# Sorted row numbers kept as integers, and two weight loads issued by another engine

## The chip, the cores and the metric

The kernel runs on one core of a Trainium2 chip. The metric is device time in microseconds of one execution. A core has five engines that each run their own list of instructions in order: TensorE (matrix products; PE in the rows, its weight loads PEld), VectorE (DVE), ScalarE (ACT), GpSimd (POOL) and SyncE (SP), which here does nothing but issue transfers and wait for their conditions. Engines meet only at semaphores. A transfer (DMA) is issued by SyncE, ScalarE or GpSimd and raises a semaphore by 16 once it has landed; 16 DMA engines carry it.

## The reference, cut to what matters

`x` is 16 sequences of 512 tokens of 128 numbers, 8192 tokens in all. Two layers follow each other:

```python
xn = layernorm(x)
x = x + cosformer_attention(xn) + moe_0(xn)        # 16 heads; shared + 16 routed experts, top 4 as a dense gate
xn = layernorm(x)
x = x + rope_causal_attention(xn) + moe_1(xn)      # 16 heads of 8; 8 experts, top 1

def moe_1(h):                                      # what the change touches
    route = softmax(h @ router_w + router_b)       # 8 experts
    best, p = argmax(route), max(route)
    for e in range(8):
        a, g = split(h @ w1[e], 2)                 # w1[e]: 128 x 1024
        y = (silu(a) * g) @ w2[e]                  # w2[e]: 512 x 128
        out = where(best == e, y, out)
    return out * p
```

## The kernel before, in words

The kernel keeps `x` on the chip and walks over the 16 sequences, called batches. A first part (up to about 540 us of the profile) computes layer 0 for each batch, the second norm, the queries, keys and values of layer 1, and the routing of layer 1. A second part (from about 580 us) computes the causal attention of layer 1 batch by batch; mixed into it run the experts of layer 1, as 71 tiles of 128 rows.

**Sorting rows to experts.** A token's row goes to one expert only, so the rows are sorted by expert in a table in memory, `xs`. A row of `xs` has 130 numbers: the 128 of the normalized token, its row number in the output (column `D`), and its probability (column `D + 1`). VectorE's `ranks` works out the place of each row (`slotu`) and writes the row numbers, which it holds in `token`, into column `D` of `xn[1]` (L1166). GpSimd's `sort` then writes 128 rows at a time with an indirect transfer, four for each batch, 64 in all (L1345). `pads` fills the ends of the experts' lists with rows of zeros (`zeros`), whose row number `NOROW` is outside the output, so that nothing is written for them. After the last of the 64 has landed, VectorE works out the tables of the tiles (`tables`, L1225 to L1257), each tile's expert and first row.

**A tile of experts**, number `n`, passes through these stages, each named by a function on the engine that does it:
- `load` on SyncE (L1500 to L1513): 128 rows of `xs` go to one of `U` = 6 buffers `xsb[:, u]`, with `u = n % 6`. From tile 6 on it first waits until the buffer is free.
- `rows` on GpSimd (L1348 to L1353): the row numbers, floats in column `D`, are cast to integers in `rowu`.
- `staged` on ScalarE copies the expert's first weights out of `w1` to `w1s`; `turned` on TensorE transposes the rows (L771), and ScalarE copies them to `xsT` (L964).
- `hidden` on TensorE (L779), ScalarE and VectorE: the first product, and silu(a) * g.
- `outputs` on TensorE (L790) with `w2`; VectorE scales by the probability into `ysb` (L1277); GpSimd adds the 128 rows to the output with an indirect transfer, the scatter, whose row numbers come from `rowu` (L1365). Its landing raises `d_ys{u}`.

**Attention.** Of each batch, `max` on TensorE and VectorE finds row maxima, group by group (four groups of four heads, counted from 0). TensorE transposes them (L721), ScalarE and VectorE split them in a high and a low half (`mrows` L924, `mlow` L1190), and SyncE's `mlow` sends both halves to the query tile with two transfers (L1447). The scores of the group wait for that (L731). ScalarE takes the exponential (L934), GpSimd masks the diagonal (L1333), TensorE multiplies by the values (L746). SyncE's `relay` (L1454 to L1476) brings the next batch's queries and keys into place, beginning with two transfers of zeros at L1468, once per batch. GpSimd's `add` adds a finished batch to the output (L1374), after as many tiles' scatters as `among(b)` says.

**The order.** Every stage has a place on a common scale, a batch taking 20 units. The places are written out by hand (`FIRST`, `SECOND`, `ATTENTION`, `CLOSING`, `END`), and those of the tile stages are derived from `tile(n)` in `LAST`: for instance `load` of tile `n + U` stands at `tile(n + 1) + 0.3` and `outputs` of tile `n` at `tile(n + 1) + 0.15`. There are nine tiles for two batches, at uneven places. `stages()` sorts all by place, and each engine runs, in that order, the stages that it has a function for. An engine that waits in one stage holds back all its later ones.

**The second experts' weights** arrive in two loads, both issued by SyncE before the change: `w1` (4 MB, at place 65.65, into the space `early` that layer 0 has used, so after its last use) and `w2` (2 MB, at place 87.5, into the space of layer 0's small tiles).

Of the kernel before, what the change touches and what calls it, by code (L numbers as in the profile page):

```python
# [13 lines left out]
U32 = mybir.dt.uint32  # L14
AX_X = mybir.AxisListType.X

P = 128
B, L, D = 16, 512, 128
# [15 lines left out]
U = 6  # L34
# [230 lines left out]
    casts=[-166.65],  # L265
    rest=[-217.1])


TPB, TBS, TB0 = 9, 2, 1
AHEAD = 5  # L270
TILES = placed(
    tile=[67.65, 76.4, 77.45, 84.2, 84.85, 87.65, 96.35, 97.4, 105.75])

# [7 lines left out]

def among(b):

    return min(NTILE, TPB * b // TBS + AHEAD)


def tile(n):
    return S2 * (TB0 + TBS * (n // TPB)) + TILES[n % TPB][0]


LAST = [(tile(n + 1) + 0.3, "load", n + U) for n in range(NTILE - U)]
LAST += [(tile(n - 1) - 0.5, "staged", n) for n in range(NTILE)] + [(tile(n - 1) + 0.3, "rows", n) for n in range(NTILE)]
LAST += [(tile(n - 1) - 0.15, "turned", n) for n in range(NTILE)] + [(tile(n), "hidden", n) for n in range(NTILE)]
LAST += [(tile(n + 1) + 0.15, "outputs", n) for n in range(NTILE)]

# [85 lines left out]
def once(names):  # L381
# [11 lines left out]
    "mean0 mean1 gated kvr kv px gate at0 x1 xl logits rope low onehot base slots mlow sub0 sub1 "  # L393
    "max heads x2 tables rowzero silu glu chain "

    "fills kept var0 var1 less0 less1 rstd0 rstd1 shift0 shift1 qs rotated rows "

    "d_x d_nextx d_big d_w d_wup d_wq d_wrest d_restx d_gate d_gates0 d_gates1 d_relayq d_relayk d_relayed d_vout d_vload d_sorted d_mrows0 d_mrows1 d_w1 d_w2 d_pad d_begun d_out"
) + [f"d_{kind}{u}" for kind in ("xs", "ys") for u in range(U)]
# [6 lines left out]
def place(nc, ctx, io):  # L406
# [101 lines left out]
    m.w2 = sb("w2", [P, E1 * FC * D])  # L508
    m.ti = sb("ti", [P, 4, E1 + 1], I32)
    m.tf = sb("tf", [P, 6, E1 + 1])  # L510
    m.rowu = sb("rowu", [P, U], U32)
    m.jr = sb("jr", [P, 4, NTAB])
    m.ji = sb("ji", [P, 3, NTAB], I32)
    m.xsb = sb("xsb", [P, U, D + 2])
# [284 lines left out]
            share[name](b, i)  # L799


def scalar_program(nc, m, s, order, work):
    act = nc.scalar

    def wk(stage, n=0):
# [142 lines left out]

    def staged(_, n):
        if n == 0:
            act.wait_ge(s["tables"], 1)
            act.wait_ge(s["d_w1"], 16)
        off = act.value_load(m.ji[0:1, 0, n:n + 1], min_val=0, max_val=(E1 - 1) * 2 * F1)
        if n >= WS:
            act.wait_ge(s["hg_mm"], n - WS + 1)
        act.copy(m.w1s[:, n % WS, :], m.w1[:, bass.ds(off, 2 * F1)]).then_inc(s["staged"], 1)  # L958
# [13 lines left out]
    def casts(_, i):  # L972
        act.wait_ge(s["d_wrest"], 16 * NWREST)
        act.copy(m.wo1[:, :], m.o16[:, :]).then_inc(s["casts"], 1)

    share = dict(casts=casts, norm0=norm0, norm1=norm1, xnT0=xnT0, kvr=kvr, up=up, q=q, kv=kv, route0=route0, gT=gT, at0T=at0T, down=down, xnT1=xnT1, parts=parts,
                 v=v, vst=vst, route1=route1, mrows=mrows, score=scores, sums=sums, mT=mT, staged=staged, turned=turned,
                 hidden=hidden)
    for name, b, i in order:
# [4 lines left out]
def vector_program(nc, m, s, order, work):  # L984
# [169 lines left out]
    def ranks(b, i):  # L1154
        ps = wk(("ranks", b, i))
        dve.wait_ge(s["ranks_mm"], b + 1)
        dve.wait_ge(s["onehot"], b + 1)
        then(dve.tensor_tensor(m.rk[:, :, :], ps[:, 0:NT * E1].rearrange("p (t e) -> p t e", t=NT),
                               m.base[:, :].unsqueeze(1).to_broadcast([P, NT, E1]), ALU.add))
        dve.tensor_tensor(m.base[:, :], m.base[:, :], ps[:, NT * E1:(NT + 1) * E1], ALU.add).then_inc(s["base"], 1)  # L1160
        then(dve.tensor_tensor(m.rk[:, :, :], m.rk[:, :, :], m.oh[:, :, :], ALU.mult))
        dve.tensor_scalar(m.token[:, :], m.token[:, :], float(L), None, ALU.add)
        then(dve.tensor_reduce(m.s1[:, 2, :], m.rk[:, :, :], AX_X, ALU.add))
        if b:
            dve.wait_ge(s["d_sorted"], 16 * NT * b)
        dve.tensor_copy(m.xn[1][:, :, D], m.token[:, :])  # L1166
        dve.tensor_copy(m.slotu[:, b * NT:(b + 1) * NT], m.s1[:, 2, :]).then_inc(s["slots"], 1)  # L1167

    def maxima(b, i):
# [118 lines left out]
def pool_program(nc, m, s, order, work):  # L1288
# [56 lines left out]
        pool.indirect_dma_start(m.xs_d, at, m.xn[1][:, t, :], None).then_inc(s["d_sorted"], 16)  # L1345


    def rows(_, n):  # L1348
        u = n % U
        pool.wait_ge(s[f"d_xs{u}"], 16 * (n // U + 1))  # L1350
        if n >= U:
            pool.wait_ge(s[f"d_ys{u}"], 16 * (n // U))
        pool.tensor_copy(m.rowu[:, u:u + 1], m.xsb[:, u, D:D + 1]).then_inc(s["rows"], 1)  # L1353

    def outputs(_, n):
        u = n % U
        pool.wait_ge(s["ycopy"], n + 1)
        pool.wait_ge(s["rows"], n + 1)
        if n == 0:
            pool.wait_ge(s["d_begun"], 16 * B)  # L1360
        gone = sum(among(b) <= n for b in range(B))
        if gone:
            pool.wait_ge(s["d_out"], 16 * gone)
        alone()
        pool.indirect_dma_start(m.out_r, bass.IndirectOffsetOnAxis(ap=m.rowu[:, u:u + 1], axis=0), m.ysb[:, u, :], None,  # L1365
                                bounds_check=B * L - 1, oob_is_err=False, compute_op=ALU.add).then_inc(s[f"d_ys{u}"], 16)

    def add(b, i):
# [7 lines left out]
    def fill(_, k):  # L1376
        if k == 0:
            pool.memset(m.px[:, :, NR0:], -1.0)
            pool.memset(m.zeros[:, :], 0.0).then_inc(s["fills"], 1)
            pool.wait_ge(s["fills"], 1)  # L1380
            pool.memset(m.zeros[:, D:D + 1], float(NOROW)).then_inc(s["fills"], 1)
        elif k == 1:
            pool.memset(m.vst[0][:, :, :, :], 0.0)
            pool.memset(m.vst[1][:, :, :, :], 0.0).then_inc(s["fills"], 1)
            pool.wait_ge(s["fills"], 3)
            for i in range(2):
                for half in range(2):
                    ones = m.vst[i][:, :, :, 16 * half + HD:16 * half + HD + 1].rearrange("p t (g j) d -> p t g j d", j=4)
                    for t in range(NT):
                        ins = pool.memset(ones[:, t, half::2, :, :], 1.0)  # L1390
            ins.then_inc(s["fills"], 1)

    share = dict(fill=fill, stats0=stats0, stats1=stats1, q=q, score=scores, rope=rope, sort=sort, add=add,
                 rows=rows, outputs=outputs)
    nothing = pool.to_reg(0.0)
    pool.memset(m.neghalf[:, :], -0.5)
    for name, b, i in order:
# [8 lines left out]
def sync_program(nc, m, s, io, order):  # L1406
# [70 lines left out]

    def w1(_, i):  # L1480
        sp.wait_ge(s["downs"], B)
        sp.wait_ge(s["gated"], (NC - 1) * B)
        sp.dma_start(m.w1, io["w1"]).then_inc(s["d_w1"], 16)

    def w2(_, i):
        sp.wait_ge(s["qk_mm"], 4 * B)
        sp.wait_ge(s["v_mm"], B)
        sp.wait_ge(s["ranks_mm"], B)
        sp.wait_ge(s["slots"], B)
        sp.wait_ge(s["d_sorted"], 16 * NT * B)  # L1490
        sp.dma_start(m.w2[:, :], io["w2"]).then_inc(s["d_w2"], 16)

    def pads(_, i):
        sp.wait_ge(s["rowzero"], 1)
        for e in range(E1):
# [4 lines left out]
    def load(_, n):  # L1500
        u = n % U
        if n == 0:
            sp.wait_ge(s["d_pad"], 16 * (E1 + 1))
            sp.wait_ge(s["tables"], 1)
            sp.wait_ge(s["v_mm"], B)
            sp.wait_ge(s["ranks_mm"], B)
            sp.wait_ge(s["d_relayk"], 48 * B)
        if n >= U:
            sp.wait_ge(s["xsT_mm"], n - U + 1)
            sp.wait_ge(s["rows"], n - U + 1)  # L1510
            sp.wait_ge(s["ycopy"], n - U + 1)
        row = sp.value_load(m.ji[0:1, 2, n:n + 1], min_val=0, max_val=E1 * CAP)
        sp.dma_start(m.xsb[:, u, :], m.xs_d[bass.ds(row, P), :]).then_inc(s[f"d_xs{u}"], 16)  # L1513
# [1 line left out]
    def rest(_, i):  # L1515
        sp.dma_start(m.X[:, 2 * NT:, :], m.x_d[:, 2:].rearrange("p b t d -> p (b t) d")).then_inc(s["d_restx"], 16)

    share = dict(rest=rest, begun=begun, mlow=mlow, vout=vout, vload=vload, gT=gT, parts=parts, relay=relayed, w1=w1, w2=w2, pads=pads, load=load)
    def consts(first, last, done):
        a, z = int(KO[first]), int(KO[last + 1])  # L1520
        sp.dma_start(m.kc[:, a:z], io["consts"][:, a:z]).then_inc(s[done], 16)
# [21 lines left out]
def program(nc, io):  # L1543
    order = stages()
    work = banks(order)
    with ExitStack() as ctx:
# [2 lines left out]
        sync_program(nc, m, s, io, order)  # L1549
        pool_program(nc, m, s, order, work)  # L1550
        vector_program(nc, m, s, order, work)
        scalar_program(nc, m, s, order, work)
        tensor_program(nc, m, s, order, work)


# [48 lines left out]
```

## Time and profile before

| | us |
|---|---|
| runs | 1335.31, 1348.19, 1355.40 |
| median | 1348.19 |
| profiled execution, whole | 1342.79 |
| its span in the trace | 1341.0 |
| TensorE busy | 1160.5 (87%) |
| VectorE busy | 938.3 (70%) |
| ScalarE busy | 849.8 (63%) |
| GpSimd busy | 544.9 (41%) |
| mean granted TensorE clock | 0.953 of full |

The span runs from the first instruction to the last; the execution's own time is 1.8 us longer. All times in the rows below are counted in microseconds from the start of the span. Busy time is the time in which an engine had an instruction in work; SyncE only issues transfers and has none. An engine's letter with a q behind it (SPq) is its sequencer, which issues transfers and handles waits. [...]

### The profile page before, as it was taken

What the parts mean: (1) busy time and instruction counts of PE and PEld (TensorE: products, weight loads), DVE (VectorE), ACT (ScalarE), POOL (GpSimd) and SP (SyncE); (2) the same over time, 40 slices, a digit from 0 to 9 for tenths busy, and PEclk for the clock granted to TensorE, in tenths of its full rate; (3) what the DMA queues carried; (4) which work ended last, traced back from release to release, by engine and by line L of the source; (5) the groups of instructions that cost most, each with busy time, mean ns of one, the idle gap of its engine ahead of it and who ended that gap; (6) DMA issues with size and microseconds to landing.
All of it is one profiled execution on the core that took longest, in us unless ns stands there. A gap on an engine that the chain in (4) does not pass through costs nothing.

```text
span 1341.0 us, 29052 instructions
## 1 busy us (share of the span) xinstructions
PE 1160.5 (87%) x9951; PEld 676.4 (50%) x9951; DVE 938.3 (70%) x2183; ACT 849.8 (63%) x1349; POOL 544.9 (41%) x888
## 2 busy tenths in 40 slices
PE   5889888999999997458989999999989999999995
PEld 2435444544445443223655665556546556555664
DVE  2457777777777776666777777777767777777752
ACT  5456766677766763135766667667666666667672
POOL 3134334433344433212454444444444435454444
PEclk9999999999999999557999999999999889899998
DMA  3634445454444444723244234414431331343112
GB/s 124 172 100 105 108 119 124 123 123 124 108 110 111 124 108 119 211 45 110 41 62 58 34 50 61 62 29 56 63 50 27 59 58 29 51 64 55 26 20 21
DMA packets 102896, 108.69 MB, mean 81 GB/s; under 512 B 13272, under 2 KB 78680, under 8 KB 102488
## 3 DMA queue, kind: packets, MB, share of 16 engines
q1 hardware_dynamic: 82032, 94.17, 30.7%
q0 software_dynamic: 20720, 12.67, 7.6%
q8 instruction: 82, 1.34, 0.4%
q14 instruction: 62, 0.51, 0.1%
HBM read 73.09 MB, written 33.10 MB: 79 GB/s over the span
## 4 chain that ended last, share of the span: by engine, by line
PE 71%; ACT 10%; DVE 8%; DMA 5%; issue 4%; POOL 1%; SPq 1%; ACTq 0%; POOLq 0%; DVEq 0%
PE PS L746 12%; PE PS L779 9%; PE PS L629 8%; PE PS L581 7%; PE PS L731 7%; ACT flow L934 6%; PE PS L790 5%; PE PS L713 5%; PE PS L607 2%; PE PS L560 2%; PE PS L573 2%; DMA qk<-gate_rows 2%; PE PS L697 2%; PE PS L771 1%; DMA early<-gate_rows 1%
## 5 line engine op out<-in xcount | busy, mean ns | idle before, releaser
L934 ACT ACTIVATE flow<-PS 128x1024 f32<-128x1024 f32 x320 | 325.2, 1023 | 140.7 <-PE PS L731 137.7
L1333 POOL TENSOR_SCALAR_AFFINE_SELECT flow<-flow 128x256 f32<-128x256 f32 (+1 forms) x448 | 226.5, 595 | 358.8 <-ACT flow L934 358.7
L1178 DVE TENSOR_REDUCE nm<-PS 128x2 f32<-128x1024 f32 x128 | 156.0, 1219 | 54.2 <-PE PS L697 53.2
L746 PE MATMUL PS<-flow 128*32 128x512 f32 (+3 forms) x2048 | 176.5, 465 | 1.3 <-POOL flow L1333 1.3
L731 PE MATMUL PS<-qk 34*128 34x512 f16 (+3 forms) x1024 | 126.8, 311 | 38.4 <-ACT flow L934 24.7
L581 PE MATMUL PS<-xnT,up 128*128 128x512 f32 x288 | 150.7, 626 | 10.5 <-ACT vtmp L901 3.2
L713 PE MATMUL PS<-qk 34*128 34x512 f16 (+3 forms) x1024 | 129.1, 314 | 34.9 <-DVE nm L1181 19.1
L1180 DVE TENSOR_REDUCE nm<-PS 128x2 f32<-128x768 f32 x128 | 122.2, 955 | 50.4 <-PE PS L697 50.3
L1365 POOL DMA_INDIRECT out_y<-ysb,rowu x71 | 113.0, 1591 | 84.3 <-DVE ysb L1277 61.3
L779 PE MATMUL PS<-xsT,w1s 128*128 128x128 f32 x1136 | 140.9, 278 | 0.0
L779 PEld LDWEIGHTS PS<-xsT,w1s 128*128 128x128 f32 x1136 | 136.6, 196 | 0.7 <-issue 0.6
L1345 POOL DMA_INDIRECT xs<-xn,slotu x64 | 69.8, 1091 | 116.1 <-DVE slotu L1167 103.8
L1184 DVE TENSOR_REDUCE nm<-PS 128x4 f32<-128x1024 f32 x64 | 78.3, 1224 | 13.0 <-PE PS L697 11.7
L746 PEld LDWEIGHTS PS<-flow 128*32 128x32 f32 x2048 | 55.1, 113 | 62.6 <-issue 39.8
L697 PE MATMUL PS<-maskb 64*128 64x128 bf16 (+1 forms) x1280 | 85.0, 211 | 0.0
L713 PEld LDWEIGHTS PS<-qk 34*128 34x128 f16 x1024 | 37.7, 95 | 93.2 <-DVE nm L1181 27.4
L790 PE MATMUL PS<-w,act 128*128 x568 | 80.4, 285 | 4.4 <-issue 3.4
L629 PE MATMUL PS<-early,down 128*128 128x512 f32 x162 | 79.9, 597 | 3.5 <-DVE early L1094 2.3
L790 PEld LDWEIGHTS PS<-w,act 128*128 128x128 f32 x568 | 68.9, 191 | 16.7 <-issue 16.7
L697 PEld LDWEIGHTS PS<-maskb 64*128 64x128 bf16 x1280 | 60.2, 99 | 29.0 <-issue 6.0
L731 PEld LDWEIGHTS PS<-qk 34*128 34x128 f16 x1024 | 36.9, 95 | 75.2 <-ACT flow L934 25.5
L958 ACT COPY w1s<-early 128x1024 f32 x71 | 74.2, 1045 | 0.3
(182 smaller groups left out, 2081.6 us busy)
## 6 DMA issues: line engine op xcount, KB each, us to landing
early<-gate_rows SPq DMA_DIRECT2D x36, 512.0 KB, 7.7
qk<-gate_rows SPq DMA_DIRECT2D x28, 512.0 KB, 8.4
qk<-relay_q SPq DMA_DIRECT2D x64, 128.0 KB
qk<-relay_k SPq DMA_DIRECT2D x64, 128.0 KB
xsb<-xs SPq DMA_DIRECT2D x71, 65.0 KB, 1.8
out_y<-X SPq DMA_DIRECT2D x16, 256.0 KB, 2.3
values<-vtmp SPq DMA_DIRECT2D x16, 256.0 KB
relay_k<-qkh SPq DMA_DIRECT2D x32, 128.0 KB, 8.8
```

What stands on the lines that cost most here:

```text
L581: pe.matmul(ps, m.up[:, c * P:(c + 1) * P], m.xnT[0][:, :], start=True, stop=True).then_inc(s["up_mm"], 1)
L629: pe.matmul(m.acc, m.down[:, c, :], m.hid[side_of(b)][:, c, :], start=(c == 0), stop=False).then_inc(s["read"], 1)
L697: ins = pe.matmul(o, m.negb[rows, side, half, :], m.eyeb[rows, :].unsqueeze(1).to_broadcast([64, len(places[k]), 64]), start=False, stop=( ...
L713: pe.matmul(ps[:, k, o:o + w], head(m.qp, b, 4 * g + h, slice(qt * P, (qt + 1) * P)), head(m.kp, b, 4 * g + h, slice(0, w)), start=(o == 0 ...
L731: ins = pe.matmul(ps[:, k, o:o + L - kt * P], head(m.kp, b, h, slice(kt * P, (kt + 1) * P)), head(m.qp, b, h, slice(kt * P, L)), start=(o ...
L746: ins = pe.matmul(m.PS[32 * j:32 * j + 32, m.PV, kt * P:], m.vst[b % 2][:, kt, 4 * g + j, :], m.pt[:, r, k * L + o:k * L + o + L - kt * P] ...
L779: ins = pe.matmul(ps[:, i * P:(i + 1) * P], m.w1s[:, n % WS, (k * FC + i) * P:(k * FC + i + 1) * P], m.xsT[:, n % 2, :], start=True, stop= ...
L790: ins = pe.matmul(ps[:, 0:D], m.act1[:, n % 2, c * P:(c + 1) * P], m.w2[:, bass.ds(off + c * D, D)], start=(c == 0), stop=(c == FC - 1))
L934: act.activation(m.pt[:, n % RING, :], m.PS[:, i:i + 2, :].rearrange("p k c -> p (k c)"), ACT.Exp, scale=1.0 / SCALE).then_inc(s["exp"], 1)
L1178: dve.tensor_reduce(nm[:, :, n, 3], ps, AX_X, ALU.max, negate=True).then_inc(s["max"], 1)
L1180: dve.tensor_reduce(nm[:, :, n - 2, 2], ps[:, :, 0:3 * P], AX_X, ALU.max, negate=True)
L1333: ins = pool.affine_select(part, part, [[0, part.shape[1]], [1, P]], ALU.is_ge, nothing, base=0, channel_multiplier=-1)
```

## The change

Row numbers are integers throughout. VectorE writes them into column `D` of the sorted rows as unsigned integers by their bits, the memset of the padding rows does the same, and the scatter takes them from the loaded rows themselves. `rows` on GpSimd, its semaphore, its stage and the tile `rowu` are gone. Since the scatter now reads column `D` of the buffer while it runs, a `load` into a used buffer waits for `d_ys{u}`, the landing of the scatter of the tile that had the buffer before; and the loads from tile 6 on stand one tile later, at `tile(n + 2) + 0.3`. `among` is written in another form. The functions `w1` and `w2` move from SyncE's program to ScalarE's, with the same waits and at the same places of the order.

```diff
-AHEAD = 5
 def among(b):
-    return min(NTILE, TPB * b // TBS + AHEAD)
+    return min(NTILE, -(-TPB * (b + 1) // TBS))

-LAST = [(tile(n + 1) + 0.3, "load", n + U) for n in range(NTILE - U)]
-LAST += [(tile(n - 1) - 0.5, "staged", n) for n in range(NTILE)] + [(tile(n - 1) + 0.3, "rows", n) for n in range(NTILE)]
+LAST = [(tile(n + 2) + 0.3, "load", n + U) for n in range(NTILE - U)]
+LAST += [(tile(n - 1) - 0.5, "staged", n) for n in range(NTILE)]

-    m.rowu = sb("rowu", [P, U], U32)

 def scalar_program(nc, m, s, io, order, work):
+    def w1(_, i):
+        act.wait_ge(s["downs"], B)
+        act.wait_ge(s["gated"], (NC - 1) * B)
+        act.dma_start(m.w1, io["w1"]).then_inc(s["d_w1"], 16)
+    def w2(_, i):
+        act.wait_ge(s["qk_mm"], 4 * B)
+        act.wait_ge(s["v_mm"], B)
+        act.wait_ge(s["ranks_mm"], B)
+        act.wait_ge(s["slots"], B)
+        act.wait_ge(s["d_sorted"], 16 * NT * B)
+        act.dma_start(m.w2[:, :], io["w2"]).then_inc(s["d_w2"], 16)

 # vector_program, ranks
-        dve.tensor_copy(m.xn[1][:, :, D], m.token[:, :])
+        dve.tensor_copy(m.xn[1][:, :, D].bitcast(U32), m.token[:, :])

 # pool_program
-    def rows(_, n):
-        u = n % U
-        pool.wait_ge(s[f"d_xs{u}"], 16 * (n // U + 1))
-        if n >= U:
-            pool.wait_ge(s[f"d_ys{u}"], 16 * (n // U))
-        pool.tensor_copy(m.rowu[:, u:u + 1], m.xsb[:, u, D:D + 1]).then_inc(s["rows"], 1)
     def outputs(_, n):
         pool.wait_ge(s["ycopy"], n + 1)
-        pool.wait_ge(s["rows"], n + 1)
...
-        pool.indirect_dma_start(m.out_r, bass.IndirectOffsetOnAxis(ap=m.rowu[:, u:u + 1], axis=0), m.ysb[:, u, :], None,
+        pool.indirect_dma_start(m.out_r, bass.IndirectOffsetOnAxis(ap=m.xsb[:, u, D:D + 1].bitcast(U32), axis=0), m.ysb[:, u, :], None,
                                 bounds_check=B * L - 1, oob_is_err=False, compute_op=ALU.add).then_inc(s[f"d_ys{u}"], 16)
     def fill(_, k):
-            pool.memset(m.zeros[:, D:D + 1], float(NOROW)).then_inc(s["fills"], 1)
+            pool.memset(m.zeros[:, D:D + 1].bitcast(U32), NOROW).then_inc(s["fills"], 1)

 # sync_program: w1 and w2 are gone
     def load(_, n):
         if n >= U:
             sp.wait_ge(s["xsT_mm"], n - U + 1)
-            sp.wait_ge(s["rows"], n - U + 1)
+            sp.wait_ge(s[f"d_ys{u}"], 16 * (n // U))
             sp.wait_ge(s["ycopy"], n - U + 1)
```

## Rows read from the trace of the kernel before

**Rows 1.** The page: share of the span in the chain of waits, by engine.

```profile
PE 71%; ACT 10%; DVE 8%; DMA 5%; issue 4%; POOL 1%; SPq 1%; ACTq 0%; POOLq 0%; DVEq 0%
```

**Rows 2.** Stretches: from:to, length, busy us of each engine (instructions), TensorE clock, DMA share, GB/s.

```profile
557.00:582.00 25.00, 6.84 (x60) 3.04 (x60) 23.17 (x48) 0.53 (x2) 0.00 (x0) 0.50 0.48 185
...
620.00:1265.00 645.00, 596.18 (x6618) 370.62 (x6617) 488.36 (x708) 436.05 (x596) 292.06 (x530) 0.98 0.33 50
```

**Rows 3.** Timeline of GpSimd: start, duration, engine, line, operation, what is written<-read, count.

```profile
784.52 1.69 POOL L1365 DMA_INDIRECT out_y<-ysb,rowu  x1 [1.27 <-issue]
...
785.54 0.87 POOL L1353 CAST rowu<-xsb 128x1 uint32<-128x1 f32 x1
...
800.55 1.57 POOL L1365 DMA_INDIRECT out_y<-ysb,rowu  x1 [0.77 <-issue]
...
1290.17 1.65 POOL L1365 DMA_INDIRECT out_y<-ysb,rowu  x1 [0.47 <-issue]
```

**Rows 4.** The chain of waits in order of time, near the end: start, duration, what.

```profile
1313.27 0.20 POOL rowu L1353
```

**Rows 5.** Who waited for the mask selections of L1333: us in total, times.

```profile
  PEld PS L746: 8.5, 29
```

**Rows 6.** SyncE's waits: who, for whom, us in total, times, longest us.

```profile
SPq L1511 <- DVE ysb L1277: 295.3, 65, 9.5
```

**Rows 7.** Landing times of the scatter of L1365, 71 of them.

```profile
DMA to landing us min/median/max: 2.7/3.3/5.1
```

**Rows 8.** Timeline of SyncE after 640 us; columns as in rows 3.

```profile
789.00 1.14 SPq L1447 DMA_DIRECT2D qk<-mrows  x2
...
808.23 2.82 SPq L1447 DMA_DIRECT2D qk<-mrows  x4
...
901.19 1.34 SPq L1468 DMA_DIRECT2D qk<-zeros  x2
...
991.52 1.35 SPq L1468 DMA_DIRECT2D qk<-zeros  x2
...
1087.25 1.35 SPq L1468 DMA_DIRECT2D qk<-zeros  x2
```

**Rows 9.** Timeline of TensorE, out of four narrow stretches; columns as in rows 3.

```profile
644.93 1.16 PE L790 MATMUL PS<-w,act 128*128 x8
...
796.92 0.68 PE L731 MATMUL PS<-qk 34*128 34x256 f16 x6
...
810.57 0.39 PE L731 MATMUL PS<-qk 34*128 34x512 f16 x2 [0.73 <-DMA qk<-mrows]
...
1306.68 0.33 PE L771 MATMUL PS<-kc,xsb 128*128 128x128 f32 x1
```

**Rows 10.** The page, transfers by line: KB each, median us from issue to landing.

```profile
xsb<-xs SPq DMA_DIRECT2D x71, 65.0 KB, 1.8
```

**Rows 11.** Timeline of SyncE, 500 to 640 us.

```profile
558.51 0.53 SPq L1483 DMA_DIRECT2D early<-in_w  x1
...
613.80 0.34 SPq L1491 DMA_DIRECT2D w<-in_w  x1
...
626.13 1.13 SPq L1447 DMA_DIRECT2D qk<-mrows  x2
```

**Rows 12.** Timeline of ScalarE, 536 to 625 us; idle time before it in brackets.

```profile
555.22 0.62 ACT L895 CAST qkh<-ra 128x512 f16<-128x512 f32 x1 [8.36 <-POOL ra L1338]
...
571.90 0.27 ACT L924 ACTIVATE mrows<-PS 16x128 f16<-16x128 f32 x1 [15.45 <-PE PS L721]
...
620.04 0.27 ACT L964 COPY xsT<-PS 128x128 f32<-128x128 f32 x1 [1.71 <-PE PS L771]
```

**Rows 13.** The chain of waits, 549 to 582 us.

```profile
555.35 2.29 DMA xs<-xn,slotu
```

**Rows 14.** Transfers from 561 to 571 us: queue, packets, MB, share of 16 engines.

```profile
q1 hardware_dynamic: 128, 3.67, 85.2%
```

**Rows 15.** Stretches: TensorE's clock around 1050 us; columns as in rows 2.

```profile
1047.10:1053.80 6.70, 6.70 (x39) 2.08 (x41) 3.02 (x4) 4.06 (x6) 2.13 (x6) 0.50 0.84 98
```

More of the change, by code:

```diff
@@ L394 @@
     "max heads x2 tables rowzero silu glu chain "
-    "fills kept var0 var1 less0 less1 rstd0 rstd1 shift0 shift1 qs rotated rows "
+    "fills kept var0 var1 less0 less1 rstd0 rstd1 shift0 shift1 qs rotated "
     "d_x d_nextx d_big d_w d_wup d_wq d_wrest d_restx d_gate d_gates0 d_gates1 d_relayq d_relayk d_relayed d_vout d_vload d_sorted d_mrows0 d_mrows1 d_w1 d_w2 d_pad d_begun d_out"
@@ L799, in tensor_program, with scalar_program @@
             share[name](b, i)
-def scalar_program(nc, m, s, order, work):
+def scalar_program(nc, m, s, io, order, work):
     act = nc.scalar
@@ L974, in casts @@
         act.copy(m.wo1[:, :], m.o16[:, :]).then_inc(s["casts"], 1)
-    share = dict(casts=casts, norm0=norm0, norm1=norm1, xnT0=xnT0, kvr=kvr, up=up, q=q, kv=kv, route0=route0, gT=gT, at0T=at0T, down=down, xnT1=xnT1, parts=parts,
+    share = dict(casts=casts, w1=w1, w2=w2, norm0=norm0, norm1=norm1, xnT0=xnT0, kvr=kvr, up=up, q=q, kv=kv, route0=route0, gT=gT, at0T=at0T, down=down, xnT1=xnT1, parts=parts,
                  v=v, vst=vst, route1=route1, mrows=mrows, score=scores, sums=sums, mT=mT, staged=staged, turned=turned,
@@ L1393, in pool_program @@
     share = dict(fill=fill, stats0=stats0, stats1=stats1, q=q, score=scores, rope=rope, sort=sort, add=add,
-                 rows=rows, outputs=outputs)
+                 outputs=outputs)
     nothing = pool.to_reg(0.0)
@@ L1476, in relayed @@
                     sp.dma_start((m.qp, m.kp)[n][b % 2][at:at + 2 * HD, :, :], src).then_inc(s["d_relayed"], 16)
[L1480 to L1491, printed above, removed]
     def pads(_, i):
@@ L1516, in rest @@
         sp.dma_start(m.X[:, 2 * NT:, :], m.x_d[:, 2:].rearrange("p b t d -> p (b t) d")).then_inc(s["d_restx"], 16)
-    share = dict(rest=rest, begun=begun, mlow=mlow, vout=vout, vload=vload, gT=gT, parts=parts, relay=relayed, w1=w1, w2=w2, pads=pads, load=load)
+    share = dict(rest=rest, begun=begun, mlow=mlow, vout=vout, vload=vload, gT=gT, parts=parts, relay=relayed, pads=pads, load=load)
     def consts(first, last, done):
@@ L1551, in program @@
         vector_program(nc, m, s, order, work)
-        scalar_program(nc, m, s, order, work)
+        scalar_program(nc, m, s, io, order, work)
         tensor_program(nc, m, s, order, work)
```

## The prediction

> **What bounds the kernel now.** I read the chain of waits by engine first: of the span of 1341.0 us, TensorE carries 71%, ScalarE 10%, VectorE 8%, transfers 5% and GpSimd 1% [rows 1]. So the engine from which the change takes work is hardly on the path. Then the stretches: from 557 to 582 VectorE is the bound (23.17 of 25 us busy, TensorE 6.84); after 620 it is TensorE again, which holds nearly everything that is left [rows 1, 2]. The change touches three places: GpSimd and SyncE in the 71 tiles of experts (from 620 to the end), the 4 MB load of `w1` in the VectorE stretch, and the 2 MB load of `w2` at 614. The profiled execution took 1342.79 us, 1.8 more than its span; the three runs shown have a median 5.4 us above it, and lie 20 us apart.
>
> **The cast leaves GpSimd.** 71 casts last 0.75 us in the middle [rows 3], but that is no price: each begins while the scatter before it still runs. The one at 785.54 ends at 786.41, and the scatter before it at 786.21 [rows 3], so a cast holds GpSimd for 0.2 us, 14 us over all 71. GpSimd lies off the path: the chain meets a cast once, at 1313.27, for 0.20 us, ahead of the mask selections that the last value products wait for [rows 4]. That is -0.2. TensorE's weight loads wait for a selection 29 times, 8.5 us in all [rows 5]; if each of those waits had a cast before it, at most 29 x 0.2 = 5.8 us could go. The chain shows only the one, so I take 0 here and keep -5.8 as an end. The casts' own waits (the load of the tile, the scatter six tiles back) are no loss either way: both are old when GpSimd comes to them.
>
> **The load's new wait on SyncE.** A load into one of six buffers now waits until the scatter out of that buffer has landed, not until its row numbers were copied, and stands one tile later in the order. Before, what it waited for last was VectorE's scaled output (65 times [rows 6]), which starts the scatter; so the wait grows by the scatter, 3.3 us from start to landing, 5.1 at most [rows 7], and the place moves by a tile. Behind it on SyncE stand the transfers of the score maxima (`mlow`), for which TensorE waits. From the order by the new places, in each batch one load stands ahead of group 3's maxima and one ahead of group 0's:
> - group 3, tightest case: the scatter starts at 784.52 [rows 3], lands at 787.8 (at most 789.6), the load's issue takes 0.4; the maxima were sent at 789.00 [rows 8]. At worst they go 1.0 us late, and the scores that need them run at 797 [rows 9]. From a first issue to the scores takes 2.3 us at group 0 (808.23 to 810.57 [rows 8, 9]), which leaves 5.7 us. Cost 0.
> - group 0, where scores follow at once: the load now ahead of it waits for the scatter of 800.55 [rows 3], landed at 803.9 (at most 805.7) plus 0.4; the maxima go at 808.23 [rows 8]. Room 3.9 us (at least 2.1). Cost 0. The other batches have this room or more.
> - the tile itself: the load of tile 69 waits for the scatter of 1290.17 [rows 3], so it can start at 1293.5 to 1295.3 and lands 1.8 us later [rows 10]; its transpose runs at 1306.68 [rows 9]. Nine us of cover remain where the wait is shortest. Cost 0.
>
> **`among`** gives the same count for every batch (9b/2 + 5 rounded down equals 9(b+1)/2 rounded up), so no output waits differently. The integer row numbers use the same VectorE copy of 128x4 and the same memset: 0.
>
> **`w2` goes to ScalarE.** SyncE issued it at 613.80 in 0.34 us [rows 11]. ScalarE comes to it before the transpose copy of 620.04, ahead of which it idles 1.71 us [rows 12]; issue and waits fit. It would leave some 4.5 us later, at about 618.3, needs 5.7 us and its start-up at the rate of [rows 14], and is first read at 644.93 [rows 9]. Its tail may now meet the maxima of batch 1, sent at 626.13 [rows 11]: 0 to 1.1 us (one piece of the size of `w1`'s, below); I take 0, since by its own length it is nearly through. SyncE loses two issues of 0.53 and 0.34 us at times when it waits for VectorE anyway: 0.
>
> **`w1` goes to ScalarE.** Here I expect a cost. ScalarE reaches it right behind the half-precision copy of 555.22 (0.62 us) and then idles 15.45 us before 571.90 [rows 12], so the issue is hidden. But the load leaves at about 555.8, not 558.51 [rows 11], while the last of the 64 scatters of rows to their experts is in flight: issued 555.35, landed 2.29 us later, and on the path, since VectorE's tables wait for it [rows 13]. `w1` moves in large pieces: 128 packets carry 3.67 MB in 10 us at 85.2% of 16 engines [rows 14], that is 16 x 8.52 / 128 = 1.1 us for each. The scatter's packets can find one such piece ahead of them, or two in turn: 0 to +2.2 us; its transfer is over quickly, so I take one, +1.1. From there to 582 VectorE has no gap to absorb it [rows 2].
>
> [...]
>
> **Sum:** 1342.79 - 0.2 + 0 + 0 + 1.1 = **1343.7** on the scale of the profiled execution; on that of the median, 1348.19 + 0.9 = 1349.1. Neither scale is better founded with 20 us between runs, so I name the middle, **1346 us**: no change.
>
> A likely cause of that spread stands in the trace. Two batches take 90.33 us (901.19 to 991.52) and the next two 95.73 us (991.52 to 1087.25) [rows 8]; in the latter TensorE's granted clock is at half, 1.2 GHz, for some 6.7 us in each batch (one of four such stretches between 999 and 1150 [rows 15]). A fall costs 5.4 / 2 = 2.7 us. The runs shown differ by seven or eight falls.
>
> **Rivals.**
> - *Slower: SyncE becomes the late one.* Place: the load ahead of group 0's maxima. If scatters landed in 10 us instead of 3.3 (they now have the loads and `mlow` beside them at other times), SyncE would be 6.7 - 3.9 = 2.8 us late in the 8 batches like the one above and, with about 1.3 us more room, 1.5 us in the other 8: +34, **1377 us**. It decides from a landing of about 7.2 us on; the longest seen is 5.1 [rows 7]. For it: these issues are followed by scores at once. 0.03.
> - *`w1` goes wholly ahead of the scatter.* Then that lands when `w1` does, 4.19 MB at 3.67 MB in 10 us [rows 14], 11.4 us after 555.8 and so 9.6 us later than now: **1352 us**. Against it, the last scatter is issued 0.4 us before `w1` and is small. [...] No row here shows a second queue beside `w1`. 0.07.
> - *Faster: GpSimd's and SyncE's waits shrink.* Selections come 0.2 us earlier at 29 waits (-5.8) and the scatter keeps its time (no +1.1): **1337 us**, and with the four clock falls gone too (-10.8) **1326 us**, 1.6% under the median. For it, 8.5 us of waits; against it, the chain holds 1% of GpSimd [rows 1]. 0.11, of which 0.04 to cross 2%.
> - *The clock falls in every batch* of the tile part: 11 more x 2.7 = +30, **1373 us**. The change shifts stretches by tenths only, so this is chance in both kernels: 0.03.
> - *The change doesn't do what it says:* the scatter may read its row numbers more slowly out of the wide loaded tile than out of a small one. Even 0.5 us for each of 71 scatters is 36 us of an engine that is busy 292 of 645 us [rows 2], and leaves 3.4 us of the room of 3.9: **1344 us**, the same answer, and counted with the forecast.
>
> **Numbers.** Forecast 0.76. The range goes from the lowest run less the GpSimd end, 1335.3 - 5.8 = 1329, to the highest plus both transfer ends and one more clock fall, 1355.4 + 2.2 + 1.1 + 2.7 = 1361, rounded to 1362, and holds the `w1` rival (1348.2 + 9.6 = 1358). Faster by over 2% 0.04 (above), slower by over 2% 0.05 (SyncE 0.03, the clock 0.02 of its 0.03, since 1373 is just under 1.02 x 1348), within 2% 0.91; 2% is about what a measurement of this kernel can tell from no change.
>
> **What would show it.** No casts on GpSimd; selections behind a scatter 0.2 us sooner. SyncE's load waiting for the scatter, and the maxima of group 0 still leaving within 0.1 us of VectorE's low half. `w1` issued before 557, the last scatter landing 3 to 4 us after its issue, and the first maxima leaving about 1 us later than 579.6 in a span otherwise the same. I am wrong if the scores of group 0 start later than 2.3 us after its maxima leave, if the stretch from 557 to 582 changes by more than 3 us, or if batches at full clock take other than 90.3 us a pair.

## The result: 0.55% slower

In 20 runs of each kernel, the changed kernel has a median of 1355.26 us (1348.71 to 1366.39) and the kernel before 1349.16 us (1335.31 to 1360.78). The ratio is 1.0055, 95% interval [1.0030, 1.0079], which is 7.4 us (4.0 to 10.7); it is not the ratio of the two medians, which lie 6.1 us apart, inside the same interval. The forecast was 1346 us and no change. The time lies inside the range, but the direction was missed: the kernel is slower by more than its measurement is uncertain, though by far less than 2%. The profiled execution took 1355.19 us, with a span of 1353.4, which is 12.4 us above that of before.

**The page after**, its first line and the chain of waits by engine:

```profile
span 1353.4 us, 28849 instructions
...
PE 73%; ACT 9%; DVE 9%; issue 4%; DMA 2%; POOL 1%; SPq 0%; ACTq 0%; DVEq 0%; POOLq 0%
```

GpSimd had 1% of the chain before [rows 1] and has 1% now, though its 71 casts are gone. The two stretches of [rows 2] in the changed kernel, with the same columns:

```profile
557.00:582.00 25.00, 5.98 (x52) 2.67 (x52) 19.25 (x38) 0.27 (x1) 0.00 (x0) 0.50 0.39 157
620.00:1265.00 645.00, 596.96 (x6546) 367.79 (x6548) 483.21 (x700) 432.55 (x590) 279.85 (x463) 0.96 0.33 52
```

In the first, VectorE works 19.25 us instead of 23.17. It waits at its beginning, and the chain of waits there says for what (start, duration, what):

```profile
554.01 7.75 DMA xs<-xn,slotu
...
561.86 0.17 DVE ti L1235
```

The last of the 64 sorting scatters lands 7.75 us after its issue, and landed after 2.29 us before [rows 13]. The transfer beside it is the subject of the next rows, ScalarE's timeline (start, duration, engine, line, operation, written<-read, count, idle time before it):

```profile
553.88 0.62 ACT L892 CAST qkh<-ra 128x512 f16<-128x512 f32 x1 [8.37 <-POOL ra L1348]
553.94 0.39 ACTq L951 DMA_DIRECT2D early<-in_w  x1
...
576.03 0.27 ACT L921 ACTIVATE mrows<-PS 16x128 f16<-16x128 f32 x1 [20.89 <-PE PS L718]
```

`w1` is issued at 553.94, 0.06 us after the start of the cast of 553.88, which runs to 554.50: ScalarE's sequencer did not wait for its end. GpSimd's and VectorE's timelines show the other side:

```profile
554.01 0.99 POOL L1355 DMA_INDIRECT xs<-xn,slotu  x1 [0.17 <-issue]
...
561.86 0.17 DVE L1235 CAST ti<-base 128x8 int32<-128x8 f32 x1 [6.63 <-DMA xs<-xn,slotu]
```

So the load was issued 0.07 us before the scatter, not 0.45 us behind it as forecast, and VectorE sat idle for 6.63 us where the same line of before reads:

```profile
557.73 0.17 DVE L1225 CAST ti<-base 128x8 int32<-128x8 f32 x1 [1.17 <-DMA xs<-xn,slotu]
```

From the scatter's issue to the tables it is 561.86 - 554.01 = 7.85 us, against 557.73 - 555.35 = 2.38 before: 5.5 us more. They are all still there at the first maxima, which SyncE sends 29.75 us after the scatter's issue (583.76, SyncE's rows below), against 579.61 - 555.35 = 24.26 before:

```profile
579.61 2.37 SPq L1447 DMA_DIRECT2D qk<-mrows  x4
```

**What the DMA engines carried** (packets, MB, share of 16 engines), in the changed kernel from 554 to 559, from 559 to 560.3 and from 560.3 to 561.5; q10 is ScalarE's queue with `w1`, q0 GpSimd's with the scatter (the two packets in the first stretch belong to the scatter before; the lines of SyncE's queue q1 are left out):

```profile
q10 hardware_dynamic: 48, 1.57, 88.4%
q0 software_dynamic: 2, 0.00, 0.0%
...
q10 hardware_dynamic: 16, 0.52, 93.3%
q0 software_dynamic: 16, 0.07, 12.4%
...
q10 hardware_dynamic: 15, 0.49, 94.8%
q0 software_dynamic: 16, 0.00, 0.8%
```

and in the kernel before from 556 to 558, when no `w1` was on its way:

```profile
q0 software_dynamic: 32, 0.07, 10.0%
```

The scatter has 16 packets with its rows (0.07 MB) and then 16 that carry next to nothing, called its closing packets here: they pass by 561.5, and it has landed at 561.76. Before, all 32 passed within 2 us. Now 48 pieces of `w1` go ahead of the rows, three for each of 16 engines if they are spread evenly, and one more for each engine goes between the rows and the closing packets. A piece occupies its engine for 16 x 1.3 x 0.933 / 16 = 1.21 us in the second stretch and for 16 x 5 x 0.884 / 48 = 1.47 us on average in the first. Four pieces are thus 4.8 to 5.9 us; the scatter's delay is 5.46 us, where the forecast had one piece.

**The rest of the 12.4 us.** I cut both spans at the last layer-0 addition to `X`, at the first copy of a finished batch to `X` and at the last such copy. Before, the first part ends at 532.03, the transition takes 121.9 us and the tile part 675.6; now these are 530.69, 129.1 and 682.2. So -1.3 + 7.2 + 6.6. The 6.6 of the tile part go with the granted clock, which was at half (a share of 0.50) for 44.2 us there and for 30.6 before. If half of such time is lost, that is 13.6 / 2 = 6.8 us, an estimate. Of the 7.2 in the transition 5.5 are the scatter. Batches at full clock take what they took: the first copy to `X` and the one two batches later stand 749.95 - 659.79 = 90.2 us apart, 743.98 - 653.94 = 90.0 before. The two tile parts in the view of stretches, before and after (the clock is the third value from the end):

```profile
653.94:1329.59 675.65, 621.97 (x6863) 390.39 (x6860) 496.26 (x726) 452.88 (x619) 309.09 (x555) 0.98 0.32 46
...
659.79:1341.97 682.18, 628.75 (x6863) 392.13 (x6861) 496.53 (x726) 452.76 (x619) 299.12 (x488) 0.97 0.31 46
```

**SyncE** did what was forecast. Its largest wait (who, for whom, us, times, longest) changed from VectorE's output [rows 6] to the scatter, with no more time in it:

```profile
SPq L1500 <- DMA out_y<-ysb,xsb: 266.9, 50, 11.9
```

In its timeline, the first line holds the first maxima of all, used above; the other two are from a batch of the tile part, two loads and the maxima of group 0 behind them. These maxima still leave 0.02 us after VectorE's low half ends, and the group's first scores start at 819.66, 2.36 us after they are sent (2.34 before [rows 8, 9]). TensorE's waits for maxima did not grow:

```profile
583.76 2.36 SPq L1449 DMA_DIRECT2D qk<-mrows  x4
...
801.04 13.08 SPq L1502 DMA_DIRECT2D xsb<-xs  x2
817.30 2.51 SPq L1449 DMA_DIRECT2D qk<-mrows  x4
```

Before, TensorE waited for maxima 16.0 us and 6.9 us in all (weight loads and products):

```profile
PEld PS L731 <- DMA qk<-mrows: 16.0, 16, 3.4
PE PS L731 <- DMA qk<-mrows: 6.9, 6, 3.3
```

and now

```profile
PEld PS L728 <- DMA qk<-mrows: 16.5, 16, 3.5
PE PS L728 <- DMA qk<-mrows: 4.0, 2, 3.3
```

### The profile page after: what moved, and what is told of

It reads as the page before. It is cut to its first block, busy times and chain, and to the rows that moved or that the text cites. A ratio compares the mean times of both kernels' runs of the same rounds, so it can differ in the third digit from the quotient of the medians.

```text
span 1353.4 us, 28849 instructions
## 1 busy us (share of the span) xinstructions
PE 1168.1 (86%) x9951; PEld 679.4 (50%) x9951; DVE 938.6 (69%) x2183; ACT 849.6 (63%) x1349; POOL 535.3 (40%) x817
## 4 chain that ended last, share of the span: by engine, by line
PE 73%; ACT 9%; DVE 9%; issue 4%; DMA 2%; POOL 1%; SPq 0%; ACTq 0%; DVEq 0%; POOLq 0%
PE PS L743 13%; PE PS L776 9%; PE PS L626 9%; PE PS L578 8%; PE PS L728 7%; ACT flow L931 6%; PE PS L787 5%; PE PS L710 5%; PE PS L557 3%; PE PS L604 2%; PE PS L570 2%; PE PS L694 2%; PE PS L768 1%; PE PS L760 1%; DVE nm L1190 1%
## 5 line engine op out<-in xcount | busy, mean ns | idle before, releaser
L743 PE MATMUL PS<-flow 128*32 128x512 f32 (+3 forms) x2048 | 182.4, 478 | 1.2 <-POOL flow L1343 1.2
L710 PE MATMUL PS<-qk 34*128 34x512 f16 (+3 forms) x1024 | 130.1, 316 | 41.2 <-DVE nm L1191 25.4
L1367 POOL DMA_INDIRECT out_y<-ysb,xsb x71 | 112.3, 1582 | 86.2 <-DVE ysb L1287 64.3
L626 PE MATMUL PS<-early,down 128*128 128x512 f32 x162 | 82.8, 617 | 3.2 <-DVE early L1104 2.1
```

The source lines that it names most:

```text
L626: pe.matmul(m.acc, m.down[:, c, :], m.hid[side_of(b)][:, c, :], start=(c == 0), stop=False).then_inc(s["read"], 1)
L710: pe.matmul(ps[:, k, o:o + w], head(m.qp, b, 4 * g + h, slice(qt * P, (qt + 1) * P)), head(m.kp, b, 4 * g + h, slice(0, w)), start=(o == 0 ...
L743: ins = pe.matmul(m.PS[32 * j:32 * j + 32, m.PV, kt * P:], m.vst[b % 2][:, kt, 4 * g + j, :], m.pt[:, r, k * L + o:k * L + o + L - kt * P] ...
```

## The experiments

The theory from these traces: the whole loss is `w1`, which reaches the DMA engines ahead of the last sorting scatter. Rivals: the integers and the moved loads of the tiles; ScalarE as issuer; the clock. Each run was timed with the kernel before on the same chip. Expectations are quoted as they were put down.

**e1, integers only.** The changed kernel with both weight loads back on SyncE:

```diff
+    def w1(_, i):
+        sp.wait_ge(s["downs"], B)
+        sp.wait_ge(s["gated"], (NC - 1) * B)
+        sp.dma_start(m.w1, io["w1"]).then_inc(s["d_w1"], 16)
```

> The integer row numbers, the scatter out of the loaded rows and the load's wait for the landed scatter, with both weight loads back on SyncE. Theory A (w1 leaves too early and holds back the last sorting scatter): the last scatter lands 2.3 us after its issue and VectorE's gap before the tables is 1.2 us, as before; time 0.995 to 1.002 of the kernel before. Theory B (the load's longer wait on SyncE costs): the whole +6 us is here, 1.0045, and group 0's maxima leave late in the batches. Theory C (ScalarE as the issuer is the cost): as before.

1351.39 us against 1350.40, ratio 1.0009 [0.9983, 1.0035]. The scatter to tables takes 2.39 us, as before. The casts, the new wait of the loads and their new place are worth nothing either way.

**e2, weights only.** The kernel before, with `w1` and `w2` issued by ScalarE:

```diff
+        act.dma_start(m.w1, io["w1"]).then_inc(s["d_w1"], 16)
```

> The kernel before with nothing but the two weight loads moved to ScalarE; casts and SyncE's old wait stay. Theory A: the last sorting scatter lands 7 to 8 us after its issue, VectorE's gap before the tables is 6 to 7 us, the first output copy of layer 1 comes 5 to 7 us late after the last sum of layer 0, and the time is 1.004 to 1.006 of before. Theory B: 1.000. Theory C: 1.004 to 1.006 too.

1356.14 us, ratio 1.0048 [1.0021, 1.0074]: the whole loss. Timelines of GpSimd, ScalarE and VectorE:

```profile
557.23 0.99 POOL L1358 DMA_INDIRECT xs<-xn,slotu  x1 [0.17 <-issue]
...
557.16 0.38 ACTq L954 DMA_DIRECT2D early<-in_w  x1
...
565.29 0.17 DVE L1238 CAST ti<-base 128x8 int32<-128x8 f32 x1 [6.85 <-DMA xs<-xn,slotu]
```

**e3, `w1` after the last scatter has landed.** The changed kernel with one more wait:

```diff
+        act.wait_ge(s["d_sorted"], 16 * NT * B)
         act.dma_start(m.w1, io["w1"]).then_inc(s["d_w1"], 16)
```

> The whole change, with w1 still issued by ScalarE but after a wait for all 64 sorting scatters to have landed (one more wait, as w2 has). Theory A: the scatter lands after 2.3 us again, w1 leaves at about 557.7 and lands by 571, 40 us before its first use; time 0.995 to 1.001 of before. Theory B: 1.0045. Theory C (the queue of ScalarE itself): stays at 1.004 to 1.006.

1348.37 us, ratio 0.9986 [0.9956, 1.0016]. The interval does not touch that of e2, with which it shared the chip. Still on ScalarE's queue, the load now costs nothing:

```profile
560.44 0.98 POOL L1356 DMA_INDIRECT xs<-xn,slotu  x1 [0.17 <-issue]
...
562.86 0.39 ACTq L952 DMA_DIRECT2D early<-in_w  x1
...
562.85 0.17 DVE L1236 CAST ti<-base 128x8 int32<-128x8 f32 x1 [1.21 <-DMA xs<-xn,slotu]
```

**e4, `w1` early, but on SyncE.** The kernel before with its place moved:

```diff
-    w1=[65.65],
+    w1=[60.9],
```

> The kernel before with one place changed: SyncE issues w1 before the last two relay transfers (place 60.9 instead of 65.65), at about 552.5, so ahead of the last sorting scatters; nothing on ScalarE. Theory A: what counts is when w1 leaves, not who issues it: the last scatter lands 5 us or more later than 2.3 us after its issue, and the time is 1.003 to 1.008. Theory C: the scatter keeps its 2.3 us and the time is 1.000.

1355.52 us, ratio 1.0049 [1.0017, 1.0080]. SyncE issued the load 2.8 us ahead of the last scatter, and VectorE waited longest of all:

```profile
549.58 0.39 SPq L1483 DMA_DIRECT2D early<-in_w  x1
...
552.40 0.99 POOL L1345 DMA_INDIRECT xs<-xn,slotu  x1 [0.17 <-issue]
...
562.03 0.17 DVE L1225 CAST ti<-base 128x8 int32<-128x8 f32 x1 [8.42 <-DMA xs<-xn,slotu]
```

Issued ahead of the scatter, `w1` costs as much from SyncE (1.0049) as it does from ScalarE (1.0048, e2): here the issuer doesn't matter, the order does.

**e5, `w1` in small pieces.** Eight transfers of 0.5 MB, 4 KB of each partition, in place of one with 32 KB:

```diff
-        act.dma_start(m.w1, io["w1"]).then_inc(s["d_w1"], 16)
+        for e in range(E1):
+            part = slice(e * 2 * F1, (e + 1) * 2 * F1)
+            act.dma_start(m.w1[:, part], io["w1"][:, part]).then_inc(s["d_w1"], 16)
```

> The whole change, with w1 issued by ScalarE at the same moment but as eight transfers of 512 KB, 4 KB of each partition instead of 32 KB in one piece. Theory A1 (the last sorting scatter takes turns with w1's pieces on each DMA engine, so its delay goes by the length of a piece): it lands 2.3 to 3.5 us after its issue instead of 7.75, VectorE's gap before the tables is 1.2 to 2.5 us, and the time is 0.998 to 1.002 of before. Theory A2 (the scatter waits for bandwidth or behind a share of the whole 4 MB): it still lands 6 us or more after its issue, and the time stays at 1.004 to 1.006.

1353.61 us against 1348.38, ratio 1.0030 [1.0000, 1.0061]. Issued as early as in e2, it cost the scatter less, though neither expectation was met (the landing lies between them):

```profile
556.98 4.54 ACTq L953 DMA_DIRECT2D early<-in_w  x8
...
557.05 0.98 POOL L1357 DMA_INDIRECT xs<-xn,slotu  x1 [0.17 <-issue]
...
562.59 0.17 DVE L1237 CAST ti<-base 128x8 int32<-128x8 f32 x1 [4.33 <-DMA xs<-xn,slotu]
```

The delay is 3.2 us instead of 5.5. From 558 to 562 us the queue moved 346 packets where the changed kernel moved some 50 in 4 us, and the scatter's 32 packets were through in that stretch:

```profile
q10 hardware_dynamic: 346, 1.29, 93.4%
q0 software_dynamic: 32, 0.07, 4.3%
```

A packet now holds its engine for 16 x 4 x 0.934 / 346 = 0.17 us, a seventh, and the delay fell by two fifths only. The size of a piece is a part of the cost, not all of it. From 557.5 to 561.15, just before the first of the scatter's rows, the load's queue moved 1.01 MB, about two of its eight transfers:

```profile
q10 hardware_dynamic: 262, 1.01, 83.4%
```

In the changed kernel 1.57 MB went ahead of the rows. And no long piece comes between the rows and the closing packets, for all 32 packets pass from 561.15 to 562. The scatter does not wait for the whole of `w1`: in the changed kernel it lands at 561.76, and `w1` at 567.1 (553.94 and 13.2 us to landing). How much of the load goes ahead of it is not one number in these traces: three large pieces for each engine and then one, or about 1 MB of small ones. Why these amounts, no run here shows.

**e6, the tiles' loads not moved.** e1, with the load's old place but its new wait:

```diff
-LAST = [(tile(n + 2) + 0.3, "load", n + U) for n in range(NTILE - U)]
+LAST = [(tile(n + 1) + 0.3, "load", n + U) for n in range(NTILE - U)]
```

> Integer row numbers with both weight loads on SyncE (e1_integers_only), but the loads from tile 6 on left at their old place, tile(n + 1) + 0.3, so that each waits for the landing of a scatter that has only just been started. My reckoning of SyncE's room: the load ahead of group 0's maxima is issued 3.3 us after its scatter's start, 0.4 us long, so the maxima leave about 1.7 us late in each of 16 batches: up to +27 us, 1.010 to 1.020, with TensorE's wait for the maxima grown by 15 us or more. If SyncE's wait does not matter even then: 0.998 to 1.003.

1412.77 us, ratio 1.0497 [1.0437, 1.0557], far more than expected. SyncE's wait for the scatter, and TensorE's for the maxima queued behind it:

```profile
SPq L1501 <- DMA out_y<-ysb,xsb: 366.3, 65, 10.8
...
PEld PS L728 <- DMA qk<-mrows: 49.0, 16, 3.4
PE PS L728 <- DMA qk<-mrows: 46.2, 15, 3.3
```

TensorE waits 95.2 us for maxima, 22.9 before. Its clock was also at half for 108.8 us of the tile part (30.6 before), so the two losses are not separated. The rival "SyncE becomes the late one" is real; against e1, which differs in this place alone, the place one tile later is what keeps it off. The new wait and the new place are one edit.

**e7, `w1` right after layer 0.** The changed kernel with `w1=[37.6]`, where I took the way for free:

> The whole change, with ScalarE's w1 at place 37.6 instead of 65.65, right after the last output of layer 0 (about 530 us), so that it is through before the last batch's four sorting scatters start at about 549. Theory A (only the overlap with the scatters costs): the last scatter lands 2.3 us after its issue, time 0.996 to 1.001. If the 4 MB also hold back the relay transfers in a way that matters, the norms or queries of the last batch come late: 1.002 to 1.006.

1352.07 us, ratio 1.0015 [0.9978, 1.0052]. A scatter stood there too, that of the batch before the last, and it met the same fate; this time ScalarE's norm of the last batch waits, since it overwrites what the scatter reads:

```profile
536.90 0.39 ACTq L951 DMA_DIRECT2D early<-in_w  x1
...
537.30 0.99 POOL L1355 DMA_INDIRECT xs<-xn,slotu  x1 [0.17 <-issue]
...
545.95 1.65 ACT L809 ACTIVATE xn<-X,shift,rstd 128x128 f32<-128x128 f32 x4 [7.92 <-DMA xs<-xn,slotu]
```

Its other input was ready at 542.94 (L1315's end), so the norm is 3.0 us late. My expectation had overlooked that scatter.

**e8, the first scores sooner.** e3, with batch 0's first maxima and scores earlier in the order:

```diff
+SOONER = {("mrows", 0): 65.0, ("mlow", 0): 65.05, ("score", 0): 67.2, ("score", 1): 67.4, ...}
```

> e3_w1_after_scatters (w1 after the scatters), and for batch 0 alone the low half of group 0's maxima and the first five score units stand ahead of most of the tables on each engine (mrows 65, mlow 65.05, scores 67.2 to 68.3). The stretch from 557 to 582 is VectorE's: TensorE and ScalarE then start the scores about 7 us sooner, at about 575 instead of 582 of the trace before. If the batch's first scores bound what follows: -3 to -6 us, 0.995 to 0.998 of before. If VectorE's tables and maxima remain the bound: no change against e3, 0.9986.

1353.62 us, ratio 1.0024 [0.9994, 1.0055]: no gain. SyncE's group of four maxima transfers began at 572.89 and was done 20.7 us later, since the second low half of VectorE came only at 592.29. The group's sending was stretched and not brought forward: a miss of mine, which says nothing of `w1`.

**e9, `w1` a little later.** The changed kernel, with ScalarE waiting for VectorE's last low half of the keys before it issues:

```diff
+        act.wait_ge(s["low"], 2 * B)
         act.dma_start(m.w1, io["w1"]).then_inc(s["d_w1"], 16)
```

> The whole change, with one more wait for ScalarE's w1: VectorE's last low half of the keys. That delays its issue by 1.3 us only, to about 1.2 us behind the issue of the last sorting scatter instead of 0.07 us ahead of it; the scatter is still in flight. Theory A3 (what counts is which transfer's pieces reach the DMA engines first): the scatter lands after 2.3 to 3.5 us and the time is 0.998 to 1.002. Theory A4 (sharing of the engines while both are in flight): it lands after 5 to 7 us and the time is 1.003 to 1.005.

1349.83 us against 1351.49, ratio 0.9981 [0.9953, 1.0010]. The load is issued 1.32 us behind the scatter, before that has landed, and costs it nothing:

```profile
562.10 0.98 POOL L1356 DMA_INDIRECT xs<-xn,slotu  x1 [0.17 <-issue]
...
563.42 0.41 ACTq L952 DMA_DIRECT2D early<-in_w  x1
...
564.54 0.17 DVE L1236 CAST ti<-base 128x8 int32<-128x8 f32 x1 [1.22 <-DMA xs<-xn,slotu]
```

The two did not meet on the DMA engines. From 562.6 to 564.4 all 32 packets of the scatter pass and none of `w1` (a queue without packets has no line):

```profile
q0 software_dynamic: 32, 0.07, 11.0%
```

**e10, tables behind a maxima reduction.** The changed kernel with `tables` at 63.4 instead of 60.95, so that VectorE has work while the scatter lands; **e11** is the same with e3's wait.

```diff
-    tables=[60.95, 63.5,
+    tables=[63.4, 63.5,
```

> The whole change, w1 as early as in it, and on VectorE the first part of the tables (the one that waits for the last sorting scatter) at place 63.4 instead of 60.95, behind two row maxima of batch 0 (2.6 us of work whose inputs are ready). If the late scatter costs through VectorE's wait alone, these 2.6 us are worked in the gap: gap down from 6.6 to about 4 us, the time 1.002 to 1.004 instead of 1.0055. If the cost lies elsewhere (transfers behind w1): still 1.005.

> e3_w1_after_scatters (w1 after all sorting scatters) together with the tables behind two maxima, so that VectorE works through the 1.2 us that it waited even before the change. Expected 1 to 2 us under e3, 0.996 to 1.000 of before: the candidate for a version that beats both, by little.

e10: 1352.37 us, ratio 1.0004 [0.9975, 1.0033]. The scatter is as late as in the changed kernel, but VectorE waits 4.44 us for it instead of 6.63, and the first maxima come 2.2 us sooner (27.55 us after the scatter's issue, not 29.75): the cost goes through VectorE's wait.

```profile
565.33 0.17 DVE L1235 CAST ti<-base 128x8 int32<-128x8 f32 x1 [4.44 <-DMA xs<-xn,slotu]
```

e11: **1347.15 us**, ratio 0.9965 [0.9931, 0.9999], the only one of twelve whose interval lies below 1, and so barely that it is no proof of a gain. In e11 VectorE comes to the tables at 560.18, 3.5 us behind the scatter's issue at 556.66, without a wait.

**e12, `w2` alone on ScalarE.** The kernel before, with `w1` left on SyncE:

> The kernel before with w2 alone issued by ScalarE, w1 on SyncE. My forecast took 0 for it, 1.1 us at most through the maxima of batch 1: 0.998 to 1.002 of before. If a second issuer's queue costs by itself: 1.003 or more.

1347.13 us, ratio 0.9973 [0.9944, 1.0001]. `w2` is free on ScalarE.

**The kernels side by side**, by their traces. `w1`: its issue, in us after the last scatter's issue. Tables and maxima: VectorE's first table operation and SyncE's first maxima, in us after the same point.

| kernel | `w1` | tables | maxima | ratio |
|---|---|---|---|---|
| before | +3.16 | 2.38 | 24.26 | 1 |
| e1 | +3.17 | 2.39 | 24.28 | 1.0009 |
| e12 | +3.16 | 2.45 | 24.35 | 0.9973 |
| e3 | +2.42 | 2.41 | 24.30 | 0.9986 |
| e9 | +1.32 | 2.44 | 24.33 | 0.9981 |
| e11 | +2.41 | 3.52 | 23.01 | 0.9965 |
| changed | -0.07 | 7.85 | 29.75 | 1.0055 |
| e2 | -0.07 | 8.06 | 29.95 | 1.0048 |
| e10 | -0.08 | 8.04 | 27.55 | 1.0004 |
| e4 | -2.82 | 9.63 | 31.52 | 1.0049 |
| e5 (small pieces) | -0.07 | 5.54 | 27.42 | 1.0030 |

Whatever else differs, the maxima are at 24.3 us where `w1` leaves at least 1.3 us behind the scatter and the tables keep their place, and at 29.8 to 31.5 where `w1` in large pieces leaves ahead of it and the tables keep their place.

## Why the forecast was wrong, by its steps

- **`w1`: the step that failed.** The term was +1.1 us, with 0 to 2.2 as its range; it measured +5.5. Two readings in it were off. First the moment: I put the load behind the end of ScalarE's cast, 0.45 us after the scatter's issue. The sequencer issues it while the cast runs, 0.07 us before the scatter. Then the amount: "one such piece, or two in turn". (The piece itself was taken a little short. In the changed kernel `w1` is 144 packets for its 4.19 MB: 128 pieces of 32 KB and 16 that carry nothing. The 3.67 MB of [rows 14] are thus 112 pieces, which give 16 x 8.52 / 112 = 1.22 us, not 1.1.) In the trace three pieces for each engine go ahead of the scatter's rows and a fourth ahead of its closing packets. How much of the miss belongs to the moment and how much to the amount is open: `w1` at 0.45 us behind the scatter was not run. The forecast had the last scatter land 3 to 4 us after its issue (7.75) and the stretch from 557 to 582 change by less than 3 us (5.5 at its end). The mechanism, pieces of `w1` ahead of the scatter's packets, was right, and so was the remark that nothing up to 582 absorbs the delay (7.85 - 2.38 = 5.5 at the tables, 29.75 - 24.26 = 5.5 at the maxima). The upper bound rested on a guess of how queues take turns, which no row showed.
- **The scale and the range.** The terms of the sum add up to +0.9 us, a slower kernel, yet the number named, 1346, lies 2.2 us under the median of 1348.19, since it averaged with the scale of one execution (1342.79). Twenty runs put the kernel before at 1349.16. That the measured 1355.26 lies inside the range is owed to the spread of single runs in it (up to 1355.4), not to the term for `w1`.
- **The rival "`w1` goes wholly ahead"** (+9.6, 1352 us) came nearer to the time than the forecast, for a reason that is half right: the load was ahead, but the scatter landed before it was through. Its chance of 0.07 rested on "the last scatter is issued 0.4 us before `w1`", the same misread moment. Both ends were at hand, and the term should have stood between 1.1 and 9.6.
- **The cast: right.** The last value products of the chain now follow a scatter without a cast, -0.2. The waits for selections stand at 8.8 us and 30 times, against 8.5 and 29 [rows 5]; the end of -5.8 was empty, and e1 agrees.

```profile
PEld PS L743 <- POOL flow L1343: 8.8, 30, 1.5
```

  That scatters read their row numbers from the wide tile more slowly did not show: a scatter holds GpSimd for 1.56 us in the middle, 1.57 before. They land in 3.3 us, as before [rows 7]:

```profile
DMA to landing us min/median/max: 2.7/3.3/4.9
```

- **SyncE: right**, cost 0, for the reasons given; e6 shows what the moved place was worth. The rival had 34 us for a late SyncE; in e6, by the old place and not by slower landings, it was 0.0497 x 1348 = 67, the clock included.
- **`w2`: right**, 0 by e12. **`among` and the integers: right**, 0 by e1.
- **The clock.** The spread of the runs was put down to falls of 2.7 us each, and the tile parts of the two traces differ so (6.6 us for 13.6 us at half clock). The traces give the clock as a share alone, 1.00 or 0.50; no run shows the 1.2 GHz that the prediction sets beside the half. The difference goes with no edit: the changed kernel has 682.2 us there, e3 and e11, which differ from it in one wait and one place of the order, 677.3 and 677.6, and e1 and e2, with disjoint halves of the change, 680.3 and 684.4.
- **Still open.** The transition takes 7.2 us more in the profiled execution, and the scatter explains 5.5. Where the scatter is on time and the tables keep their place, the transition takes 121.8 to 124.3 us (e12, the kernel before, e9, e3, e1), and where it is late 127.8 to 130.1 (e2, the changed kernel, e4). So the remaining 1.7 us lie within what executions differ by. Half-clock time there was 88.8 us in the changed kernel and 78.4 before; no run separates it. Nor did a run settle how a DMA engine divides its time between a load and a scatter.

## What to carry to other kernels

Before moving a bulk load, find the small transfer on the path that is in flight at its new place, and compare the two issue times, taking the load's from the moment at which its engine's sequencer is free, not from the end of the instruction before it (here 553.94, and not 554.50). Here a load that left first cost the small one four of its pieces. A wait for that transfer in front of the load, which had slack, turned 1.0055 into 0.9986 here (e3). The new wait on SyncE, behind which other transfers stand, was free where its place moved as well (e1, 1.0009); where it did not, the ratio was 1.0497, the clock included (e6).

## What the runs showed of the hardware

- **The order of issue decides, within about a microsecond.** `w1` issued 0.07 us ahead of the scatter delays it 5.5 us (the changed kernel, 7.85 against 2.38 to the tables); 1.32 us behind, it delays it by less than 0.1 us (2.44 against 2.38), and its packets come only after the scatter's (e9). Where between the two the cost vanishes was not tried.
- **A head start of 2.8 us costs only 1.8 us more** (e4 against the changed kernel, 9.63 and 7.85): in neither did the scatter wait for the whole load, which took 13.2 us from issue to landing in the changed kernel and 16.7 us in e4.
- **ScalarE's sequencer issued the load beside ScalarE's own running instruction**: in the changed kernel at 553.94 in a cast of 553.88 to 554.50, and in e2 at 557.16 in the same cast, begun at 557.10.
- **The scatter's closing packets waited as well:** all 16 pass one piece of `w1` after its rows (560.3 to 561.5). e2 has the same counts of pieces, 48 ahead of the rows and 16 beside them.
- **Another small transfer paid as well:** in the changed kernel the low half of the keys (128 KB), issued by SyncE behind `w1`, lands after 11.5 us instead of 2.4. No wait for it stands in either trace.

```profile
relay_k<-qkl SPq DMA_DIRECT2D x1, 128.0 KB, 11.5
```
